# Attention scores in row tiles: three passes of 32 rows in place of one stack of 97, the shift moved into the exponential, row sums inverted in turned form

## What is computed

```python
qkv = jnp.einsum('bnd,ed->bne', x, w_qkv)
q, k, v = jnp.split(qkv, 3, axis=-1)
q, k, v = (to_heads(q), to_heads(k), to_heads(v))
dots = jnp.einsum('bhnd,bhmd->bhnm', q, k) * SCALE
attn = jax.nn.softmax(dots, axis=-1)
out = jnp.einsum('bhnm,bhmd->bhnd', attn, v)
...
x = _layernorm(x + _L0_attn_ref(x, L0_attn_w_qkv, L0_attn_w_out, L0_attn_b_out), axis=-1)
```

## Time and profile before

| | us |
|---|---|
| median of three runs | 2046.24 (2042.54 to 2047.2) |
| the profiled execution, its own time | 2044.68 |
| its span, first to last instruction | 2042.9 |
| `project`, up to the barrier | 0 to about 312 |
| `attend` | 312 to about 1519 |
| all later stages | 1519 to 2042.9 |

### The profile page before, as it was taken

The page is one execution under the profiler, slowest core; times in us unless marked ns, Lnnn a source line. Parts: engine busy times, 40 slices in busy tenths (PEclk is TensorE's granted clock), DMA queues, the critical chain, the costliest instruction groups (busy, mean ns, idle before and its releaser), DMA issues. The chain is left out here.

```text
span 2042.9 us, 31283 instructions
## 1 busy us (share of the span) xinstructions
PE 1910.2 (94%) x10398; PEld 936.1 (46%) x10398; DVE 1656.2 (81%) x1461; ACT 1422.3 (70%) x1593; POOL 106.5 (5%) x67
## 2 busy tenths in 40 slices
PE   8999996999999999999999999999958998699786
PEld 6777772333333333333333333333325775344332
DVE  4434436999999999999999999999963776688687
ACT  5444535888888888888888888888843655465465
POOL 0000000000000000000000000000002210000164
PEclk9999997999999999999999999999988997799898
DMA  7655647124133132142151151150146530123174
GB/s 274 231 191 212 223 178 164 43 54 99 36 78 84 37 87 65 37 96 58 35 120 42 35 118 37 42 120 26 42 106 208 174 126 18 43 128 170 63 281 160
DMA packets 114410, 221.70 MB, mean 109 GB/s; under 512 B 9576, under 2 KB 28136, under 8 KB 112764
## 3 DMA queue, kind: packets, MB, share of 16 engines
q1 hardware_dynamic: 110332, 212.23, 34.6%
q10 hardware_dynamic: 3968, 7.86, 1.0%
HBM read 134.61 MB, written 85.46 MB: 108 GB/s over the span
## 5 line engine op out<-in xcount | busy, mean ns | idle before, releaser
L698 ACT ACTIVATE probs<-scores 128x1024 f32<-128x1024 f32 x1024 | 993.5, 1022 | 187.8 <-PE scores L801 187.7
L762 DVE TENSOR_TENSOR dve_sum<-dve_sum,probs 128x2048 f32<-128x2048 f32 x384 | 880.0, 2292 | 12.0
L801 PE MATMUL scores<-q_stack,k_stack 97*128 97x512 f32 x2054 | 617.0, 422 | 26.8 <-DMA v_group<-v_scratch 18.2
L801 PEld LDWEIGHTS scores<-q_stack,k_stack 97*128 97x128 f32 x2054 | 345.7, 188 | 503.4 <-ACT probs L698 415.0
L842 PE MATMUL mixed_ps<-probs,v_group 128*32 128x512 f32 x4096 | 545.5, 605 | 0.0
L842 PEld LDWEIGHTS mixed_ps<-probs,v_group 128*32 128x32 f32 x4096 | 80.5, 108 | 188.7 <-issue 188.7
L333 DVE TENSOR_TENSOR parts<-proj_ps,parts 128x512 fp32r<-128x512 f32 x64 | 44.1, 690 | 94.4 <-ACT parts L263 94.4
L1194 PE MATMUL mix_y_ps<-w_out_parts,mix_o_in 128*128 128x512 f32 x384 | 98.5, 411 | 22.3 <-DMA mix_o_in<-o_scratch 22.3
L720 DVE RECIPROCAL row_inverse<-mixed_ps 128x512 f32<-128x512 f32 x33 | 110.8, 3357 | 6.2 <-PE mixed_ps L815 5.0
L411 PE MATMUL proj_ps<-x_hi,qkv_hi 128*128 128x512 f32 x256 | 102.2, 399 | 9.9 <-DVE qkv_lo L322 9.9
L1710 PE MATMUL down_y_ps<-down_t,down_ints 128*128 128x512 bf16 x352 | 85.2, 407 | 21.9 <-DVE down_ints L1619 21.9
(11 more groups left out here) (184 smaller groups left out, 1715.6 us busy)
## 6 DMA issues: line engine op xcount, KB each, us to landing
k_stack<-k_scratch SPq DMA_DIRECT2D x108, 256.0 KB
q_stack<-q_scratch SPq DMA_DIRECT2D x99, 256.0 KB
o_scratch<-out_parts SPq DMA_DIRECT2D x33, 512.0 KB, 3.0
h_scratch<-h SPq DMA_DIRECT2D x6, 2816.0 KB, 8.1
h<-h_scratch SPq DMA_DIRECT2D x6, 2816.0 KB, 10.9
k_scratch<-parts SPq DMA_DIRECT2D x32, 512.0 KB, 6.6
q_scratch<-parts SPq DMA_DIRECT2D x32, 512.0 KB, 2.7
mix_o_in<-o_scratch SPq DMA_DIRECT2D x32, 512.0 KB, 7.9
```

The costliest lines, as they stand in the source:

```text
L698: nc.scalar.activation(probs[n % P_SLOTS][:, pair * 2 * CH:(pair + 1) * 2 * CH], scores[e % S_SLOTS][:], ACT.Exp, scale=SCALE).then_inc(pr ...
L762: nc.vector.tensor_tensor(total[:], first[:], probs[n % P_SLOTS][:], ALU.add).then_inc(dve_added, 1)
L801: last = nc.tensor.matmul(scores[e % S_SLOTS][:, j * CH:(j + 1) * CH], k_stack[:, h, k * P:(k + 1) * P], q_stack[c % 2][:, h, :], start=Tr ...
```

## The change

Scores: `attend` no longer stacks rows. `k_parts` and `q_parts` hold the high and the low part of four heads, head `h` on partitions 32h to 32h+31. For a block, PE issues three passes (`TERMS`) of four matmuls of 32 rows each, one a head, that add up in PSUM; the four of a pass stand in the four row quarters of the array and write four banks. One wait stands ahead of all twelve and one signal (`scores_done`) behind them. PE is two blocks ahead (`AHEAD`) where it was three pairs ahead.

Shift: the extra row is gone. `project` makes the largest query norm of each chunk and head as well, spreads the product of bounds over the partitions with one matmul, and keeps it as `keep.shift`; `attend` copies eight columns of it once a turn, and the exponential takes them as its bias. The stores and loads of norm rows are gone.

Sums: three blocks of a chunk stay unadded (13 additions become 12), their sums follow block 1. The sums are turned in 32x32 squares, so that one reciprocal of 128x16 does, which is then spread and turned back.

The 97-row form lives on as `attend_exact`, which is skipped as the second `attend` was.

```diff
-                for b in range(BATCH):
-                    dst = scr.k_row[:, b * SEQ:(b + 1) * SEQ].rearrange("h (c t) -> h c t", t=CH)
-                    sp.dma_start(dst, shift_row[:, b].bitcast(F32).unsqueeze(1).broadcast_to([HEADS, CPB, CH])).then_inc(shift_out, 16)
                 for r in range(RING):
...
-                        act.wait_ge(chunk_done, 1 + n + 1)
-                        act.wait_ge(row_out[u], 1 + 16 * i)
-                        nc.scalar.activation(q_norm[u][:], q_norm_ps[:], ACT.Sqrt).then_inc(q_row_done, 1)
-                act.wait_ge(k_bound_done, 1)
-                nc.scalar.activation(k_bound[:], k_bound[:], ACT.Sqrt, scale=1.02).then_inc(k_root_done, 1)
+                act.wait_ge(bound_done, 1)
+                nc.scalar.activation(bound[:], bound[:], ACT.Sqrt, scale=1.02).then_inc(root_done, 1)
...
-                        nc.vector.tensor_reduce(k_most[:, bass.ds(n, 1)], k_norm_ps[:], AX.X, ALU.max).then_inc(k_max_done, 1)
-                v.wait_ge(k_max_done, 1 + NCH)
-                nc.vector.tensor_reduce(k_bound[:], k_most[:].rearrange("h (b c) -> h b c", b=BATCH), AX.X, ALU.max).then_inc(k_bound_done, 1)
+                        nc.vector.tensor_reduce(most[:, 0, bass.ds(n, 1)], k_norm_ps[:], AX.X, ALU.max).then_inc(norm_max_done, 1)
+                        nc.vector.tensor_reduce(most[:, 1, bass.ds(n, 1)], q_norm_ps[:], AX.X, ALU.max).then_inc(norm_max_done, 1)
+                v.wait_ge(norm_max_done, 2 + 2 * NCH)
+                nc.vector.tensor_reduce(k_most[:], most[:, 0].rearrange("h (b c) -> h b c", b=BATCH), AX.X, ALU.max).then_inc(k_most_done, 1)
+                v.wait_ge(k_most_done, 1)
+                nc.vector.tensor_tensor(bound[:].rearrange("h (b c) -> h b c", b=BATCH), most[:, 1].rearrange("h (b c) -> h b c", b=BATCH),
+                                        k_most[:].unsqueeze(2).broadcast_to([HEADS, BATCH, CPB]), ALU.mult).then_inc(bound_done, 1)
...
+                v.wait_ge(root_done, 1)
+                nc.vector.tensor_tensor(bound_diag[:], keep.ident[0:HEADS, 0:HEADS].unsqueeze(1).broadcast_to([HEADS, NCH, HEADS]),
+                                        bound[:].unsqueeze(2).broadcast_to([HEADS, NCH, HEADS]), ALU.mult).then_inc(bound_diag_done, 1)
+                v.wait_ge(spread_done, 1)
+                nc.vector.tensor_reduce(bound_pairs[:], out_ps[1][:, 0:NCH * HEADS].rearrange("p (n j) -> p n j", j=2), AX.X, ALU.max).then_inc(pairs_done, 1)
+                v.wait_ge(pairs_done, 1)
                 for b in range(BATCH):
-                    nc.vector.tensor_scalar(shift_row[:, b], zeros[:], k_bound[:, b:b + 1], None, ALU.subtract).then_inc(shift_done, 1)
+                    nc.vector.tensor_scalar(keep.shift[:].rearrange("p (g b c r) -> p b c g r", b=BATCH, c=CPB, r=HPG // 2)[:, b],
+                                            bound_pairs[:].rearrange("p (b c g r) -> p b c g r", b=BATCH, c=CPB, r=HPG // 2)[:, b],
+                                            HEADROOM / SCALE, -SCALE, ALU.max, ALU.mult)
...
     PIECES = 4
     KPP = KB // PIECES
+    RAW_BLOCKS = range(KB - 3, KB)
+    ADDS = KB - len(RAW_BLOCKS) - 1
+    W_SLOT = 4
+    SUMS_AT = 1
+    AHEAD = 2
+    TERMS = ((0, 0), (0, 1), (1, 0))
...
+                def load_kv(g, b, piece):
+                    t0 = b * SEQ + piece * KPP * P
+                    cols = slice(piece * KPP * P, (piece + 1) * KPP * P)
+                    keys = scr.k[bass.ds(g, 1), :, :, bass.ds(t0, KPP * P)].rearrange("g s p t -> p (g s) t")
+                    sp.dma_start(k_parts[:, :, cols].bitcast(F32), keys).then_inc(kv_in[piece], 16)
+                    vals = scr.v[bass.ds(t0, KPP * P), bass.ds(g * P, P)].rearrange("(k p) c -> p k c", p=P)
+                    sp.dma_start(v_group[:, piece * KPP:(piece + 1) * KPP, :], vals).then_inc(kv_in[piece], 16)
...
+                with act.Fori(0, ITERS) as it:
+                    act.wait_ge(probs_done, (it + 1) * EXPS)
+                    nc.scalar.activation(shift[:].rearrange("p c r -> p (c r)"), keep.shift[:, bass.ds(it * (CPB * PAIRS), CPB * PAIRS)], ACT.Copy,
+                                         bias=HEADROOM).then_inc(shift_done, 1)
+                    act.wait_ge(shift_done, it + 1)
...
+                            before = n - P_SLOTS
+                            chunk, block_in = it * CPB + before // KB, before % KB
+                            if block_in in RAW_BLOCKS:
+                                act.wait_ge(sums_done, chunk + 3)
+                            else:
+                                act.wait_ge(dve_added, (chunk + 1) * ADDS + max(block_in, 1))
+                            act.wait_ge(scores_done, 1 + it * BLOCKS + n + 1)
+                            for pair in range(PAIRS):
+                                nc.scalar.activation(probs[n % P_SLOTS][:, pair * 2 * CH:(pair + 1) * 2 * CH], scores[(n * PAIRS + pair) % S_SLOTS][:],
+                                                     ACT.Exp, bias=shift[:, c, pair:pair + 1],
+                                                     scale=SCALE).then_inc(probs_done, 1)
...
+                    v.wait_ge(inverse_done, f)
+                    nc.vector.transpose(turned[:].rearrange("p c j -> p (c j)"), mixed_ps[u][:]).then_inc(sums_read, 1)
+                    v.wait_ge(sums_read, 1 + f + 1)
+                    v.wait_ge(extremes_done, 2 + 2 * f)
+                    v.wait_ge(widened, f)
+                    nc.vector.reciprocal(turned_inverse[:], turned[:, :, 0]).then_inc(inverse_done, 1)
+                    v.wait_ge(inverse_done, f + 1)
+                    v.wait_ge(turned_back, f)
+                    nc.vector.tensor_copy(inverse_wide[:], turned_inverse[:].unsqueeze(2).broadcast_to([P, COLS, HD])).then_inc(widened, 1)
+                    for at, op in zip(extreme, (ALU.max, ALU.min)):
+                        nc.vector.tensor_tensor(at[:], at[:], turned_inverse[:], op).then_inc(extremes_done, 1)
+                    v.wait_ge(widened, f + 1)
+                    v.wait_ge(normal_done, 1 + f)
+                    nc.vector.transpose(inverse[:], inverse_wide[:].rearrange("p c j -> p (c j)")).then_inc(turned_back, 1)
...
+                    v.wait_ge(turned_back, f + 1)
+                    v.wait_ge(lo_done, 2 + f - 1)
+                    nc.vector.tensor_tensor(normal[u][:], mixed[:], inverse[:], ALU.mult).then_inc(normal_done, 1)
+                    v.wait_ge(normal_done, 1 + f + 1)
+                    v.wait_ge(stored[u], 1 + it * (16 * CPB // 2) + 16 * (c // 2))
+                    nc.vector.tensor_copy(out_parts[u][:, 0, :], normal[u][:]).then_inc(hi_done, 1)
+                    v.wait_ge(hi_done, f + 1)
+                    nc.vector.tensor_tensor(out_parts[u][:, 1, :], normal[u][:], out_parts[u][:, 0, :].bitcast(F32),
+                                            ALU.subtract).then_inc(lo_done, 1)
...
+                    back, user = max((slot_user(n * PAIRS + pair, S_SLOTS, EXPS) for pair in range(PAIRS)), key=lambda at: (-at[0], at[1]))
+                    pe.wait_ge(probs_done, (it + 1 - back) * EXPS + user + 1)
+                    for t, (a, b) in enumerate(TERMS):
+                        for h in range(HPG):
+                            rows = slice(h * HD, (h + 1) * HD)
+                            last = nc.tensor.matmul(scores[(n * PAIRS + h // 2) % S_SLOTS][:, h % 2 * CH:(h % 2 + 1) * CH],
+                                                    k_parts[rows, a, k * P:(k + 1) * P], q_parts[c % 2][rows, b, :],
+                                                    start=t == 0, stop=t == len(TERMS) - 1)
+                    last.then_inc(scores_done, 1)
...
+                def finish(it, c):
+                    u = (c + 1) % 2
+                    pe.wait_ge(mixed_copied, it * CPB + c + 1)
+                    pe.wait_ge(raw_filled, len(RAW_BLOCKS))
+                    parts = [probs[k % P_SLOTS] for k in RAW_BLOCKS] + [dve_sum[u]]
+                    for p, part in enumerate(parts):
+                        if part is dve_sum[u]:
+                            pe.wait_ge(dve_added, (it * CPB + c + 1) * ADDS)
+                        for j in range(HPG):
+                            last = nc.tensor.matmul(mixed_ps[u][j * HD:(j + 1) * HD, :], keep.ones[:, 0:HD], part[:, j * CH:(j + 1) * CH],
+                                                    start=p == 0, stop=p == len(parts) - 1)
+                    last.then_inc(sums_done, 1)
...
+                            n = c * KB + k
+                            score(it, n + AHEAD)
```

More of the change, by code:

```diff
@@ L440, in _ @@
                 last.then_inc(row_done, 1)
+                pe.wait_ge(bound_diag_done, 1)
+                nc.tensor.matmul(out_ps[1][:, 0:NCH * HEADS], keep.ones[0:HEADS, :], bound_diag[:].rearrange("h b k -> h (b k)"),
+                                 start=True, stop=True).then_inc(spread_done, 1)
 def true_max(nc, scr, keep):
@@ L612, in _ @@
             def _(sp):
```

(15 more changed lines are left out.)

277 lines of the change are left out of this document (219 added, 58 removed).

## The result

The changed kernel takes **2106.02 us** (median, 2101.18 to 2109.49) against 2045.45 of before on the same chip: ratio 1.0296 (1.0271 to 1.0320). In brackets stand the lowest and highest time, and behind a ratio its 95% interval. The forecast was slower by 10, and the kernel is slower by 60: the direction and the mechanism (a closed chain of scores and exponentials) held, and one term of the chain, the length of an exponential, did not.

What follows compares the result with a forecast made beforehand. PE's own work bounded the kernel before, with DVE almost as full; afterwards a chain of scores and exponentials would decide. Chain +1, turn's end +14, start -6 made +9, so 2056 against 2046.2; forecast's own range 2020 to 2075, widened to 2000 to 2130.

Steps and rivals of the forecast that it cites:

- The chain: In `attend`, a block's scores, one exponential and the next scores form a closed chain of 2.08 a block, against 2.12 before.
- The step that failed: The exponential on the chain in `attend` was put at 1.02, from 1.94 for two with 0.92 between starts.
- A pass: Four score matmuls of 32 rows in different row quarters take 0.23 together, the pace of one f32r matmul.
- rivals 2 and 3: Score passes' weight loads: not hidden behind the pass before, 2110, chance 0.13; or quarters' loads one after another, 2266, chance 0.05.
- rival 2: Loads of a score pass don't hide behind the pass before: each pass 0.33, chain 2.18, total 2110; chance 0.13.
- the rule on loads: Trainium skill, cited for score passes: a weight load overlaps running matmuls only in another row group.
- The rule of 3.07 times for four row tiles: Skill's speedup for four row tiles of 512 columns, not four times; gives 0.30 a score pass and 2129 in all.
- Sums: PE's sums in a chunk grow by two groups, from 2.58 to 3.44; the block with the sums takes 5.3.
- DVE: DVE's work in a chunk of `attend` falls from 36.4 to about 32.7, 4 us short of binding.
- Rival 4: DVE transposes in the sums are dear, 3.36 each: DVE needs 38 a chunk and binds, 2103; chance 0.05.
- The turn's end: ACT's table load and copy add 1.43, PE's branch 2.25: 3.7 instead of 1.6, +14 over seven ends.
- The start: Ahead of the first scores, fewer waits and 3 transfers instead of 9 save between 3 and 8 us; 6 taken.

Runs made afterwards that it cites:

- Run 5: Changed kernel with the last of the three score passes of a block left out; 2014.33 us, ratio 0.9850 to the kernel before.
- runs 7 and 8: Changed kernel with scores stacked again, one 96-row matmul a head, a wait and signal per pair; three unadded blocks 2063.98 us, two unadded blocks 2040.08 us.
- run 1: Changed kernel with the column of shifts taken off the exponential and a quarter of the scale; 2063.34 us, ratio 1.0092 to the kernel before.
- run 2: Changed kernel with two key blocks unadded instead of three; 2078.65 us, ratio 1.0165 to the kernel before.
- run 11: Changed kernel with stacked scores, two unadded blocks and TensorE's loop as four rounds of two turns; 2038.62 us, ratio 0.9968 to the kernel before.
- run 9: Changed kernel with another order of the three score tiles, first pairs on tile 0, second pairs on 1 and 2 in turn; 2109.39 us, ratio 1.0312.

## Why the prediction was right or wrong

**The chain.** Right, and closed as described: 0.05 from the exponential's end to the load, passes 0.23 apart, 0.44 from the last matmul to the exponential. Run 5 shows that it decides, runs 7 and 8 that nothing else of the change makes a chunk longer than PE's work. ACT's idle time is 0.07 a block and not 0.1 to 0.2, as its exponentials are longer.

**The step that failed** is the chain's last term, "one exponential: 1.94 for two with 0.92 between their starts, so 1.02". It was read from instructions without a bias column, and the change gives every exponential one. It is 1.11. The term is short by 0.09, which is 15 x 32 x 0.09 = 43 us, and run 1 gives back 43. The other terms of the chain are together short by 0.02, another 10 us: the first pass takes 0.34 and not 0.33, and the rest is rounding. The Trainium skill states the price (ScalarE: Activation LUTs, What ACT_TABLE_LOAD costs: each operand of one value a partition adds about 93 ns); 1.023 against 1.112, 89 ns, agrees with it. I had listed no edit for ACT but the copy at a turn's head. An operand that is new on an instruction of the critical chain is a part of the change like any other, and with it the forecast would have been 2056 + 43 = 2099 (the forecast's own sum gives 2055.3 and not 2056).

**A pass.** Right at 0.23, with four row tiles side by side and each load hidden behind the pass before: rivals 2 and 3 don't occur. The four loads of a pass, 0.18 each, run side by side as well: twelve of them keep PEld busy for 0.54. That rival 2's sum, 2110, lies close to the measured 2106 is luck twice over. Its passes of 0.33 don't occur, and it is added up wrongly: with two passes 0.10 dearer the chain is 2.28 and not 2.18, the chunk 39.7, and the time 2157. The matmuls of 0.21 that the forecast sets against the rule on loads stand in no row of its own; 0.21 is half of a group's 0.43. What answers the rule is the timeline, loads of 0.19 under matmuls that start 0.23 apart. The rule of 3.07 times for four row tiles isn't borne out: four take as long as one of the earlier trace rows does, so an estimate of 0.30 a pass was too dear.

**Sums.** Right: a chunk less its 15 blocks is 38.18 - 15 x 2.19 = 5.3, and run 2 shows that two groups of 0.43 come off it one to one.

**DVE.** Right: 32.0 busy in a chunk against the 32.7 forecast, which took its terms off the chunk's 36.4 and not off DVE's 35.89; off those it is 32.2. Rival 4 does not occur.

**The turn's end.** Forecast +14, measured +17, with the sizes of its parts off and partly cancelling, so that the closeness is in part luck. The timeline of the changed kernel at the end of the first turn, which answers to the earlier trace rows, and the branch's row:

```profile
466.85 0.98 PE L827 MATMUL scores<-q_parts,k_parts 32*128 32x512 f32 x12 [0.23 <-ACT probs L706]
...
470.05 0.97 PE L827 MATMUL scores<-q_parts,k_parts 32*128 32x512 f32 x12 [1.22 <-ACT probs L706]
470.10 1.28 ACT L688 ACT_TABLE_LOAD   x1
...
471.82 4.31 ACT L706 ACTIVATE probs<-scores,shift_now 128x1024 f32<-128x1024 f32 x4 [0.21 <-ACT shift_now L688]
...
472.99 0.97 PE L827 MATMUL scores<-q_parts,k_parts 32*128 32x512 f32 x12 [0.97 <-ACT probs L706]
...
476.78 0.97 PE L827 MATMUL scores<-q_parts,k_parts 32*128 32x512 f32 x12 [1.83 <-ACT probs L706]
```

```profile
L857 PEldq COMPARE_BRANCH  x8: 83/3446/4917, 473.2 to 1569.7; - x8
```

From 466.85 to 472.99 are two blocks in 6.14 instead of 4.38: ACT's part is 1.76, forecast 1.43. The next block takes 3.79 instead of 2.19: TensorE's branch is 1.6, forecast 2.25. The forecast counted eight matmuls of the program in the queue when the branch starts; the trace shows twelve. The branch starts at 473.2 and takes 3.43, and behind its start PE still starts the block's second and third pass and its values, 1.8 of work until 474.95 instead of 1.3. At three of the seven ends the clock falls behind the branch's wait, which costs 1.2 each, and at one the branch takes 4.9, 1.5 over its median, and PE stands for 3.47. Windows of the changed kernel at its second end:

```profile
631.16:633.16 2.00, 0.41 (x4) 0.38 (x8) 1.65 (x2) 1.01 (x2) 0.00 (x0) 0.94 0.44 81
633.16:635.16 2.00, 2.00 (x20) 0.56 (x12) 1.34 (x1) 0.85 (x1) 0.00 (x0) 0.50 1.02 344
635.16:637.16 2.00, 2.00 (x24) 0.68 (x20) 0.60 (x1) 1.27 (x2) 0.00 (x0) 0.70 0.66 225
```

The forecast had no such term: before, PE stands once at each end, for 1.1 to 1.5, and its clock stays at 1.00. How the 1.6 of a turn's end before divides between table load and branch the forecast left open; run 11, whose scores are stacked as they were before, gives the branch 0.3.

**The start.** Forecast -6 with bounds of 3 to 8, measured -9 in this pair of executions. The first transfer was issued at 305.79 instead of 312.03, -6.2, and the first scores came 7.9 behind it instead of 10.4, -2.6. The size of the first part is not settled by one pair. Over the nine kernels with row tiles the first copy starts between 319.0 and 323.6, and in the two with the old start at 327.2 and 329.4, so the start gives between 4 and 10; a forecast of 6 with bounds of 3 to 8 fits that. The fewer transfers alone give 2.3 to 4.3: 6.2 to 8.1 from the first transfer to the first scores instead of 10.4.

**The sum** with the measured terms: chain and sums +55 instead of +1, ends +17 instead of +14, first and last chunk +1, start -9 instead of -6, behind the last copy -1.5. What stays open is why three of the seven ends lose the clock and four don't: at six of them the waits ahead are alike, and the seventh, with the longest wait of all, 3.47, keeps its clock.

## What to carry to other kernels

Before a wait is merged or a tile shape changed, write down the chain that the new waits close, and price every instruction on it as it will be, with its new operands and not as it stands in the old trace. The same 90 ns cost nothing where TensorE's work decides and 43 us where a chain does. Work taken off an engine that nobody waits for buys nothing, and what it is traded for (two groups of sums a chunk, 27 us) is paid in full.

## What the runs showed of the hardware that was not expected

- A bias column makes an exponential of 128x1024 longer, 1.023 to 1.112 us, with zeros in it too. The distance between the starts of two grows from 0.92 to 1.005 in run 5, where ACT is the limit; each takes 1.15 there.
- Four matmuls of 32 rows and 512 columns in different row quarters start together, and such passes follow each other at 0.23, which is what one matmul of 97 rows takes. Their weight loads, four at a time, are hidden behind the pass before.
- Idle time of TensorE is not only lost, and how it was divided mattered here. At a turn's end of the changed kernel PE stands for 1.2, 1.0 and 1.7 to 1.9; the clock fell to 0.50 at three of seven ends, each time behind the third wait and never behind the first two. In run 9 the first two are one wait of 1.98, and the clock fell behind it at six of seven ends, at four of them for longer. A longer wait alone does not settle it: the 3.47 at one end of the changed kernel was followed by no fall.
- TensorE's branch back over a long body took 3.4 us in the median of eight and 4.9 at most. It costs 1.6 of that, and 3.3 at most, where one block of scores and values is queued ahead of it.
